# Causal attention with an expert layer: the first half's transposes stand most of a slot later, and block transposes, normalisations and copies come in another order

## What is computed

```python
def attn(x, w_kv_down, w_kv_up, w_q, w_out):          # x: 8 x 1024 x 256, 16 heads of 64
    latent_kv = x @ w_kv_down                         # rank 128
    k, v = split(latent_kv @ w_kv_up)
    q = x @ w_q
    att = softmax(mask_causal(q @ k.T / 8))
    return (att @ v) @ w_out
x = layernorm(x + attn(x, ...))
x = layernorm(x + expert_choice_ffn(x, ...))          # 8 experts, top 257 tokens of 1024 each
```

## Time and profile before

| | us |
|---|---|
| median of 3 runs | 3476.64 |
| lowest, highest | 3470.68, 3477.32 |
| the profiled execution, its own time | 3472.87 |
| its span | 3471.0 |
| TensorE busy in it | 2987.7 (86%) |
| VectorE busy | 1971.3 (57%) |
| ScalarE busy | 1776.9 (51%) |
| GpSimd busy | 1568.1 (45%) |

### The profile page before, as it was taken

How to read it: one execution, slowest core, us unless ns; L and a number is a source line. 1 busy time by engine, 2 the same in 40 slices (tenths; PEclk the granted TensorE clock), 3 DMA queues, 4 the chain that set the end, 5 groups by cost and what they waited for, 6 DMA issues and landing times. The chain is left out here.

```text
span 3471.0 us, 53404 instructions
## 1 busy us (share of the span) xinstructions
PE 2987.7 (86%) x17196; PEld 1986.9 (57%) x17196; DVE 1971.3 (57%) x4808; ACT 1776.9 (51%) x3981; POOL 1568.1 (45%) x1661
## 2 busy tenths in 40 slices
PE   7788888887888887888888888885998999999997
PEld 4444444443444444444444444443998999999997
DVE  4555555555555555555555555554397885455446
ACT  5555555555555555555555555553544444444443
POOL 2334334333333433433343333331676777666665
PEclk9899899899898999899999998997999999999998
DMA  4886886887778777877877868878774444444335
GB/s 119 215 226 187 220 225 189 221 215 207 207 205 223 204 202 223 214 196 210 230 187 214 229 184 225 217 193 242 268 258 139 119 100 106 104 106 101 78 73 150
DMA packets 345525, 644.62 MB, mean 186 GB/s; under 512 B 36360, under 2 KB 244616, under 8 KB 337056
## 3 DMA queue, kind: packets, MB, share of 16 engines
q1 hardware_dynamic: 303200, 590.68, 61.4%
q0 software_dynamic: 25152, 33.75, 5.8%
q10 hardware_dynamic: 16896, 16.78, 1.4%
HBM read 347.38 MB, written 293.69 MB: 185 GB/s over the span
## 5 line engine op out<-in xcount | busy, mean ns | idle before, releaser
L209 POOL TENSOR_SCALAR prob<-prob,inv 128x128 f32<-128x128 f32 (+7 forms) x1024 | 748.9, 745 | 1485.0 <-DVE inv L657 1485.0
L651 DVE CUSTOM_DVE_ANT_0 s_ps<-s_ps,mask 128x128 f32<-128x128 f32 (+7 forms) x1024 | 756.6, 771 | 985.1 <-PE s_ps L330 985.1
L514 ACT ACTIVATE prob<-s_ps,neg_max 128x128 f32<-128x128 f32 (+7 forms) x1024 | 755.3, 739 | 820.3 <-DVE neg_max L651 820.3
L358 PE MATMUL s_ps<-ident,prob 128*128 128x128 f32 x1280 | 237.8, 313 | 357.6 <-POOL prob L209 357.6
L665 DVE STREAM_TRANSPOSE squares<-prob 128x640 f32<-128x640 f32 (+3 forms) x512 | 500.1, 1015 | 2.1 <-DMA s_d<-squares 2.1
L376 PE MATMUL o_ps<-late_t,v 128*64 128x512 f32 (+3 forms) x2048 | 414.5, 526 | 46.2 <-DMA late_t<-s_d 45.5
L358 PEld LDWEIGHTS s_ps<-ident,prob 128*128 128x128 f32 x1280 | 155.6, 152 | 445.9 <-issue 408.8
L330 PE MATMUL s_ps<-tok 64*128 64x512 f32 (+3 forms) x1536 | 344.9, 556 | 10.3 <-ACT tri L532 7.3
L330 PE MATMUL s_ps<-k,q 64*128 64x512 f32 (+3 forms) x1536 | 344.1, 554 | 10.6 <-ACT tri L532 7.8
L1670 PE MATMUL e_y<-w_hi,hid_hi 128*128 128x256 f32 (+1 forms) x1088 | 312.1, 287 | 0.0
L1672 PE MATMUL e_y<-w_hi,hid_lo 128*128 128x256 f32 (+1 forms) x1088 | 308.2, 283 | 0.0
(11 more groups left out here) (233 smaller groups left out, 5545.1 us busy)
## 6 DMA issues: line engine op xcount, KB each, us to landing
s_d<-squares SPq DMA_DIRECT2D x64, 1024.0 KB, 5.1
late_t<-s_d SPq DMA_DIRECT2D x256, 256.0 KB, 6.9
s_d<-squares SPq DMA_DIRECT2D x64, 896.0 KB, 7.0
late_t<-s_d SPq DMA_DIRECT2D x256, 224.0 KB, 6.6
s_d<-squares SPq DMA_DIRECT2D x64, 768.0 KB, 4.0
late_t<-s_d SPq DMA_DIRECT2D x256, 192.0 KB, 6.9
s_d<-squares SPq DMA_DIRECT2D x64, 640.0 KB, 2.9
late_t<-s_d SPq DMA_DIRECT2D x256, 160.0 KB, 5.1
```

What stands on the lines that cost most here:

```text
L209: pool.tensor_scalar(pr, pr, inv[:, i:i + 1], 1.0, ALU.mult, ALU.mult).then_inc(norm_done, 1)
L358: mm = pe.transpose(turned_part(n, q, h)[:, to * P:(to + 1) * P], prob[(2 * q + h) % PB][:, j * P:(j + 1) * P], ident[:])
L514: act.activation(prob[i][:, 0:(q + 1) * P], score_part(n, s), ACT.Exp, scale=-1.0, bias=neg_max[:, i:i + 1], accum_out=total[:, i:i + 1]). ...
L651: dve.tensor_tensor_reduce(part, part, mask[:, T - (q + 1) * P:T], 1.0, -MASKED, ALU.add, ALU.min, neg_max[:, i:i + 1]).then_inc(max_done, 1)
```

## The change

No operation is added or taken away. On TensorE, `turn(n, 0)` moves from slot 1 to slot 2, behind the scores of block 2 and `project_v` half 1, and `turn` 1, 2, 3 move one place back as well; `project_q` half 1 moves from slot 5 to slot 4. On ScalarE the copies of turned tiles and the keeps follow. On GpSimd the normalisation of block 7 comes after that of the next pair's block 0, and `weights_low` after block 1; `normal` gives the semaphore count that goes with that order. On VectorE the reciprocals stand before the second maximum of their slot, and the transposes of blocks 4 and 5 move one slot forward, those of block 6 back behind the maxima of block 1.

```diff
--- before.py
+++ after.py
@@ -166,6 +166,11 @@
         def y_place(n, g):
             return min(2 * n + 3, 2 * NPAIRS) if g else max(2 * n, 1)
 
+
+        def normal(n, q, h):
+            place = {0: max(8 * n - 1, 0), 7: min(8 * n + 8, 8 * NPAIRS - 1)}.get(q, 8 * n + q)
+            return 2 * place + h + 1
+
         def last_of_batch(n):
             return n % NPAIR == NPAIR - 1 and n < NPAIRS - 1
 
@@ -230,15 +235,20 @@
             weights_low(0)
 
             def slot(n, q):
-                norm(n, q)
+                if q < 7:
+                    norm(n, q)
+                if q == 0 and n:
+                    norm(n - 1, 7)
+                if q == 1 and n + 1 < NPAIRS:
+                    weights_low(n + 1)
                 for i in x_pieces(n, q):
                     x_low_part(n // NPAIR + 1, i)
-                if q == 0 and n + 1 < NPAIRS:
-                    weights_low(n + 1)
-                if last_of_batch(n) and q in (2, 3):
-                    l_low_part(n // NPAIR + 1, q - 2)
+                if last_of_batch(n) and q == 2:
+                    for i in range(2):
+                        l_low_part(n // NPAIR + 1, i)
 
             over_pairs(slot)
+            norm(NPAIRS - 1, 7)
 
         @block.sync
         def _(sp):
@@ -352,7 +362,7 @@
                 elif n:
                     pe.wait_ge(exp_done, 16 * n)
                 for h in range(2):
-                    pe.wait_ge(norm_done, 16 * n + 2 * q + h + 1)
+                    pe.wait_ge(norm_done, normal(n, q, h))
                     for j in range(q + 1):
                         to = q - j if h else j
                         mm = pe.transpose(turned_part(n, q, h)[:, to * P:(to + 1) * P],
@@ -464,33 +474,33 @@
                     if n >= 2:
                         pv(n - 2, 1, [6, 7])
                     project_v(n, 0)
-                    turn(n, 0)
                 if q == 2:
                     project_v(n, 1)
-                    turn(n, 1)
+                    turn(n, 0)
                 if q == 3:
                     if last_of_batch(n):
                         project_l(n // NPAIR + 1, 0)
-                        turn(n, 2)
+                        turn(n, 1)
                         project_q(n + 1, 0)
                     else:
                         if after:
                             project_q(n + 1, 0)
-                        turn(n, 2)
+                        turn(n, 1)
                 if q == 4:
                     if last_of_batch(n):
                         project_l(n // NPAIR + 1, 1)
-                        turn(n, 3)
+                        turn(n, 2)
                         project_k(n + 1, 0)
                     else:
                         if after:
                             project_k(n + 1, 0)
-                        turn(n, 3)
+                        turn(n, 2)
                     if after:
                         project_k(n + 1, 1)
-                if q == 5:
+                    turn(n, 3)
                     if after:
                         project_q(n + 1, 1)
+                if q == 5:
                     pv(n, 0, range(4))
                 if q == 6 and n:
                     pv(n - 1, 1, [0, 1, 2])
@@ -596,38 +606,38 @@
                 if q == 2:
                     if n >= 2:
                         copy_y(n - 2, 1)
-                    copy_turned(n, 0)
                     exp(n, 4)
                     copy_v(n, 1)
                     exp(n, 5)
                 if q == 3:
-                    copy_turned(n, 1)
+                    copy_turned(n, 0)
                     exp(n, 6)
                     if new:
                         l_split(n // NPAIR + 1, 0)
                     exp(n, 7)
                 if q == 4:
                     if new:
-                        copy_turned(n, 2)
+                        copy_turned(n, 1)
                     if after:
                         keep(n + 1, 0)
                     if new:
                         l_split(n // NPAIR + 1, 1)
+                        copy_turned(n, 2)
+                        keep(n + 1, 1)
                     else:
-                        copy_turned(n, 2)
+                        copy_turned(n, 1)
                         if after:
                             keep(n + 1, 1)
+                        copy_turned(n, 2)
+                    if after:
+                        keep(n + 1, 2)
                     exp(n, 8)
                     copy_turned(n, 3, [0])
-                    if new:
-                        keep(n + 1, 1)
                     exp(n, 9)
                 if q == 5:
                     if after:
-                        keep(n + 1, 2)
+                        keep(n + 1, 3)
                     exp(n, 10)
-                    if after:
-                        keep(n + 1, 3)
                     exp(n, 11)
                 if q == 6:
                     copy_y(n, 0)
@@ -656,10 +666,10 @@
                 dve.wait_ge(exp_done, 16 * n + 2 * q + 2)
                 dve.reciprocal(inv[:, i:i + 2], total[:, i:i + 2]).then_inc(inv_done, 1)
 
-            def turn_squares(n, q):
+            def turn_squares(n, q, heads=range(2)):
                 t = q + 1
-                for h in range(2):
-                    dve.wait_ge(norm_done, 16 * n + 2 * q + h + 1)
+                for h in heads:
+                    dve.wait_ge(norm_done, normal(n, q, h))
                     if h == 0:
                         dve.wait_ge(squares_out[q % 2], 16 * (2 * n + (q - 4) // 2))
                     dve.transpose(square_all(q).rearrange("p (j h k c) -> p j h k c", j=4, h=2, c=Q)[:, :, h, :, :],
@@ -690,18 +700,21 @@
                                   ALU.subtract).then_inc(l_low, 1)
 
             def slot(n, q):
-                maximum(n, 2 * q)
                 if q == 3:
                     invert(n, 2)
-                if q == 5:
-                    invert(n, 4)
+                if q == 7:
+                    turn_squares(n, 5)
+                maximum(n, 2 * q)
+                if q > 4:
+                    invert(n, q - 1)
                 maximum(n, 2 * q + 1)
-                if q == 0 and n:
-                    turn_squares(n - 1, 6)
                 if q == 1:
                     if n:
                         invert(n - 1, 7)
+                        turn_squares(n - 1, 6, [0])
                     invert(n, 0)
+                    if n:
+                        turn_squares(n - 1, 6, [1])
                 if q == 2:
                     invert(n, 1)
                     if n:
@@ -710,12 +723,8 @@
                     invert(n, 3)
                 if q == 4:
                     copy_turned_last(n)
-                if q == 6:
-                    invert(n, 5)
+                if q == 5:
                     turn_squares(n, 4)
-                if q == 7:
-                    invert(n, 6)
-                    turn_squares(n, 5)
                 if n == NPAIRS - 1 and q < 4:
                     wo_low(q)
```

## The result

| | before | after |
|---|---|---|
| median of 3 runs, us | 3476.64 | 3295.12 |
| lowest, highest | 3470.68, 3477.32 | 3293.47, 3303.16 |
| the profiled execution, its own time | 3472.87 | 3295.12 |
| an ordinary pair (mean of 53) | 36.34 | 34.35 |
| a pair at a change of batch (mean of 7) | 41.52 | 33.49 |

The ratio is 0.9489, with a 95% interval of 0.946 to 0.9518. The forecast was 3372 us, faster; the range of 3250 to 3450 holds the result. The means in the table leave out the first two ordinary pairs and the last one. Between the first and the last T (start of a pair's first scores) lie 2150 us where there were 2320: 170 of the profiled execution's 177.8 us went there, 2.03 in each of 56 ordinary pairs and 8.0 in each of 7 changes of batch. TensorE's wait for the last pair's transfers shrank by 3.7 us (26.45 to 22.72).

The account below looks back on a forecast made before the run. Bound: TensorE's stall before the first transposes, with the DMA chain right behind it. 56 ordinary pairs x (36.46 − 35.1) = 76 us plus 25 at changes of batch, 101 together, gave 3372 us; range 3250 to 3450.

Parts of the forecast that it names:

- The bound: Ordinary pair: the DMA chain takes all 36.0 us; TensorE's chain reaches `late_t` within 0.3 us of the landing.
- Point 1: TensorE's first transposes: 4.93 us stall goes; waits of 0.5 us before project_v half 1 and 1.6 before project_q come.
- Point 2: TensorE's clock behind the first transposes: no half clock there, saving 2.35 us; through block 6's scores at T + 24.4.
- Point 3: VectorE: moved transposes and reciprocals cost nothing; block 6's transposes end at T + 6.1, against 6.6.
- Point 4: GpSimd: block 7's transposes end near T + 9.7 instead of T + 15.5; `l_lo` order delays block 3's turn in 7 pairs.
- Point 5: ScalarE: copies of turned tiles behind the projections' keeps; no wait over 0.2 us, costed at nothing.
- Point 6: DMA: read 4 out of write 6's way saves 2.5 us; write 6 to landing 21.2 us, landing T + 27.3, pair 33.0.
- Point 7: The new 2.9 us wait at `late_t` loses TensorE's clock: 0 to 2.35 us per pair, taken as 2.1; pair 35.1.
- Rival A: Clock stays up at `late_t`: 33.0 us a pair, 219 us less, 3254; chance 0.15.
- Rival B: DMA keeps pace and TensorE is the bound: 30.1 us a pair, 381 us less, 3092; chance 0.06.
- C: The stall only moves: project_q waits for `w_lo` as long as block 0 was waited for; time within 0.2%; chance 0.04.
- D: Slower: transfers overlapped anyway, so 2.5 us are not gained; 37.85 us a pair, 53 us more, 3526; chance 0.10.

Follow-up runs that it names:

- e1: Kernel before with only TensorE's and ScalarE's new order, VectorE's and GpSimd's kept old: 3472.88 us, ratio 0.9996.
- e11: Kernel before with only VectorE's new order; GpSimd, TensorE and ScalarE as before: 3273.23 us, ratio 0.9421.
- e2: Kernel before with only VectorE's and GpSimd's new order, TensorE's and ScalarE's kept old: 3349.11 us, ratio 0.9633.
- e5: Changed kernel with write 5, and so read 4, held back until the exponentials of the next pair's block 0: 3504.93 us, ratio 1.0088 to the kernel before.
- e6: Changed kernel with GpSimd making `w_lo` before it scales block 1 instead of behind it: 3349.87 us, ratio 0.9652 to the kernel before.
- e7: Changed kernel with read 5 before write 6 and `w_lo` before block 1 together: 3107.43 us, ratio 0.8946 to the kernel before.
- e10: Changed kernel with `w_lo` made before block 1 is scaled, plus three unused filler products before `late_t`: 3246.02 us, ratio 0.9338 to the kernel before.
- e4: Changed kernel with three unused filler products on TensorE before the `late_t` products, ordinary pairs only: 3259.80 us, ratio 0.9393 to the kernel before.
- e3: Changed kernel with read 5 queued before write 6 on the DMA queue: 3116.70 us, ratio 0.8956 to the kernel before.

## Why the prediction was right, and where not

- **The bound (two chains within 0.3 us): right.** In e1 TensorE is ready for `late_t` 3.5 us sooner (T + 26.9 instead of 30.4) and the landing moves by 0.7 only: nothing gained. VectorE's list moves the landing from 30.7 to 27.7 and gives the time.
- **Point 1: right.** The stall is gone; project_q waits 1.95 us on `w_lo` (1.6 forecast). The 0.5 us before project_v half 1 is not there in ordinary pairs. TensorE is ready for `late_t` at 27.60 − 2.67 = T + 24.9 (24.4).
- **Point 2: half right.** No half clock behind the first transposes, but one that I had not counted stands behind the wait for `w_lo` (914 to 917 in the pair shown, 0.50), in 29 of the 44 pairs. It lies in TensorE's slack and shortens the wait at `late_t`: that was 0.73 to 2.90 us in these 29 pairs, 12 of which lost the clock there, and 3.23 to 4.60 us in the other 15, of which 14 lost it.
- **Point 3: the time is right, the comparison wrong.** Block 6's transposes end at T + 5.9 (6.1 forecast), but in the kernel before they ended at T + 5.9 too (1011.09 + 2.10 in the earlier trace rows). The T + 6.6 that I set against it is when write 6 left, and it left right behind the issuing of read 4 (1011.34 + 2.42). So the 0.6 us were gained on the queue, by read 4's new place, and not by VectorE finishing sooner.
- **Point 4: times right, worth wrong.** Block 7's end at T + 9.3 and write 7 leaves at T + 9.75 (9.7 and 9.8), but e11 shows that this brings the landing nothing. The `l_lo` order, which I thought would cost at a change of batch, does so only in TensorE's old order (e2).
- **Point 5: right in ordinary pairs.** 3.2 us in all before the transposes, 7.4 before project_v in 8 places, the longest 1.1, where I had expected none over 0.2.
- **Point 6: right.** 21.6 us from write 6 to landing (21.2), T + 27.6 (27.3). e5 bears out the reason in part: of the 2.5 us it shows 1.7 as read 4's bytes, and 0.9 more as write 6 waiting for read 4 to be issued. The DMA share of the stage rises from 0.79 (300 to 2300 us) to 0.85 (300 to 2100).
- **Point 7: the size of one loss was right, its frequency wrong.** From `late_t` to T takes 6.81 us on average against 5.65: 1.16 x 44 / 26 = 1.96 us for each pair that lost the clock, where I took 2.1 for all. It was lost in 26 of 44. My upper bound of 2.35 was too low as well: in 8 of the 44 pairs more was lost, up to 2.92 (8.57 against 5.65), as in the pair at 938.71 shown above, whose twelve products took 5.39 us (8.56). The pair was forecast at 35.1 and is 34.35. The account of HAM oscillation in the Trainium skill's "TensorE: Matmul & The Clock Gate", of a loop whose DMA wait puts the clock down on every pass, fits e6 (43 of 44 pairs) and e5 (44), not the changed kernel (26).
- **The lengths before: misread.** I took 36.46 and 39.9 us from the first transposes of one pair to those of another, so the 1.2 us by which the last pair of a batch stalls longer (6.17 against 4.93) went to the seven pairs ahead. From T to T they are 36.34 and 41.52. With 36.34 the forecast's own terms give 69 us for the ordinary pairs, not 76.
- **The change of batch: the term furthest off for its size.** Forecast 3.5 us each, 25 together; measured 8.0, 56. The whole pair at 1152.60 before and the one at 1074.85 after, as stretches of before and of after:

```profile
1152.60:1193.74 41.14, 32.84 (x164) 17.27 (x162) 20.54 (x50) 22.94 (x54) 20.12 (x23) 0.92 0.70 178
```

```profile
1074.85:1108.26 33.41, 30.62 (x164) 16.27 (x162) 20.91 (x50) 22.36 (x54) 20.08 (x23) 1.00 0.78 202
```

```profile
1093.74 0.49 PE L436 MATMUL j_ps<-w_hi 128*128 128x512 f32 x1 [1.07 <-POOL w_lo L232]
...
1102.61 2.79 PE L386 MATMUL o_ps<-late_t,v 128*64 128x512 f32 x12
```

TensorE's same 164 pieces take 2.2 us less at a clock of 1.00 instead of 0.92: a price of the stall that I had left out. Its idle time falls from 8.3 us to 2.8, since few waits take the stall's place (the longest is 1.07), and there is none before `late_t`, where the extra work covers the landing. I had put 1.6 us of new waits and a cost of `l_lo` there.

The sum redone: 56 x 2.03 = 114 (76 forecast), 7 x 8.0 = 56 (25), 3.7 at the tail and 4 elsewhere, 178 against 101. The direction and the two chains were right; the gain is 1.8 times the forecast, because the clock stayed up in 18 of 44 pairs, where I had charged its loss to all, and because I had priced the change of batch too low. Rival A was where the clock is always kept: e11 is that case, at 33.3 us a pair (33.0). Rival B did not happen; even in e7 the landing comes last in ordinary pairs. Rivals C and D did not happen; e5 comes to D's 37.85 us a pair (37.7), but because read 4 is back in front of write 6, not because the transfers overlapped anyway.

Not tried: VectorE's list in its parts, and GpSimd's on top of the kernel before. Why the clock is kept behind some waits and lost behind others of equal length (in the changed kernel kept up to 3.23 us, lost from 1.91 on) stays open.

## What to carry to other kernels

Find the chain that lands last and look at what stands in front of its first transfer; here nothing else shortened an ordinary pair until that was moved. Then look for stretches with a DMA share near 0.00 while a ready transfer stands in an in-order queue behind one that waits: two lines swapped there gave as much again as the whole change. Before speeding up an engine that only waits longer for it, count what the longer wait does to TensorE's clock: it can turn a gain into a loss.

## What was unexpected

- Shortening a wait off the path by about 1 us cost 55 us (e6), and the same edit with the clock held gained 14 (e10). With landings within 0.5 us of each other, mean waits of 0.5 and 0.8 us lost no clock (e4, e11), 1.42 lost it in 4 pairs, 2.6 to 2.7 in 24 to 26, and 4.14 in 43.
- Leaving TensorE's, ScalarE's and GpSimd's lists as they were gave 3273.23 us, 22 less than changing them too, though TensorE then waits 148.6 us in 106 places from 300 to 2100 before its transposes.
- The 1024 KB write landed in 8.0 us after the change and in 5.4 us in e3, with the same bytes in a pair: its landing depends on what is queued around it.
